# Attention on Trainium2: values of a head pair in one tall matmul, and a new order of the steps on TensorE

## The reference

```python
q, k, v = (split_heads(x @ W) for W in (W_query, W_key, W_value))
scores = einsum('hbqd,hbkd->hbqk', q, k)        # 64 x 64 for each sequence and head, not scaled
out = einsum('hbqk,hbkd->hbqd', softmax(scores), v)
return relu(merge_heads(out) + x @ W_res)       # [2048, 64, 128]
```

## Time and profile before

| | before |
|---|---|
| median of 3 runs | 1635.06 us |
| the profiled execution | 1633.92 us |
| its span (first to last instruction) | 1632.1 us |
| TensorE matmul busy | 1606.5 us, 98% of the span |
| TensorE weight load busy | 1541.2 us, 94% |
| VectorE, ScalarE, GpSimd busy | 1200.2, 1096.1, 932.6 us |
| granted TensorE clock over the span | 0.994 |

### The profile page before, as it was taken

The page is one execution under the profiler, slowest core; times in us unless marked ns, Lnnn a source line. Parts: engine busy times, 40 slices in busy tenths (PEclk is TensorE's granted clock), DMA queues, the critical chain, the costliest instruction groups (busy, mean ns, idle before and its releaser), DMA issues.

```text
span 1632.1 us, 95535 instructions
## 1 busy us (share of the span) xinstructions
PE 1606.5 (98%) x41984; PEld 1541.2 (94%) x41984; DVE 1200.2 (74%) x1537; ACT 1096.1 (67%) x1794; POOL 932.6 (57%) x1290
## 2 busy tenths in 40 slices
PE   6999999999999999999999999999999999999997
PEld 6999999999999999999999999999999999999996
DVE  4677777777777777777777777777777777777774
ACT  3676666667676766666676767666676767666664
POOL 2555555565655555565656555555656555555655
PEclk9999999999999999999999999999999999999998
DMA  2222222222223222222222232222222222322221
GB/s 59 76 83 89 83 85 84 84 84 84 84 84 88 83 87 84 84 84 84 84 84 86 83 89 83 86 84 84 84 84 84 84 88 82 88 84 84 84 84 54
DMA packets 271797, 135.33 MB, mean 83 GB/s; under 512 B 9312, under 2 KB 271712, under 8 KB 271712
## 3 DMA queue, kind: packets, MB, share of 16 engines
q1 hardware_dynamic: 270336, 134.25, 28.0%
q10 hardware_dynamic: 1376, 0.26, 0.1%
HBM read 67.37 MB, written 67.11 MB: 82 GB/s over the span
## 4 chain that ended last, share of the span: by engine, by line
PE 98%; issue 1%; DVE 0%; ACTq 0%; DMA 0%; ACT 0%; POOLq 0%; POOL 0%; DVEq 0%
PE ps_so L242 17%; PE ps_pt L231 16%; PE ps_so L220 13%; PE ps_qk L196 8%; PE ps_qk L198 8%; PE ps_qk L197 8%; PE ps_vr L209 8%; PE ps_vr L210 7%; PE ps_vr L211 7%; PE ps_x L186 7%; DMA w_raw<-in_L_rec_W_res_dram 0%; ACTq L334 0%; POOLq L39 0%; DVE attn L378 0%; DVE x_lo L351 0%
## 5 line engine op out<-in xcount | busy, mean ns | idle before, releaser
L150 POOL TENSOR_TENSOR y<-attn,vr 128x256 f32<-128x256 f32 x512 | 341.4, 688 | 596.3 <-issue 585.2
L308 ACT COPY probs_t<-ps_pt 128x512 f32<-128x512 f32 x512 | 302.0, 590 | 423.3 <-PE ps_pt L231 423.2
L362 DVE TENSOR_REDUCE row_max<-ps_so 128x16 f32<-128x1024 f32 x256 | 313.5, 1225 | 339.7 <-PE ps_so L242 339.5
L156 POOL TENSOR_SCALAR y<-y 128x512 f32<-128x512 f32 x256 | 380.7, 1487 | 22.4
L292 ACT COPY qk<-ps_qk 128x512 f32<-128x512 f32 x512 | 301.1, 588 | 65.0 <-PE ps_qk L198 13.9
L196 PE MATMUL ps_qk<-x_hi,w_hi 128*128 128x256 f32 x1024 | 332.7, 325 | 5.6 <-DVE x_lo L351 3.3
L231 PE MATMUL ps_pt<-ident,probs 128*128 128x128 f32 x2048 | 323.2, 280 | 0.8 <-ACT probs_t L308 0.7
L300 ACT COPY vr<-ps_vr 128x512 f32<-128x512 f32 x512 | 297.8, 582 | 33.8 <-PE ps_vr L211 1.5
L367 DVE TENSOR_TENSOR shifted<-ps_so,row_max 128x1024 f32<-128x1024 f32 x256 | 313.5, 1225 | 8.8
L209 PE MATMUL ps_vr<-w_hi,x_hi 128*128 128x256 f32 x1024 | 310.8, 304 | 0.1
L242 PE MATMUL ps_so<-vr,probs_t 64*64 64x33 f32 x8192 | 293.0, 222 | 4.2 <-issue 2.8
(11 more groups left out here) (23 smaller groups left out, 2249.0 us busy)
## 6 DMA issues: line engine op xcount, KB each, us to landing
x_in<-in_r_x_dram SPq DMA_DIRECT2D x256, 256.0 KB, 2.8
out_dram<-y SPq DMA_DIRECT2D x256, 256.0 KB, 2.3
w_raw<-in_L_rec_W_query_dram ACTq DMA_DIRECT2D x1, 64.0 KB, 3.1
w_raw<-in_L_rec_W_key_dram ACTq DMA_DIRECT2D x1, 64.0 KB, 3.7
w_raw<-in_L_rec_W_value_dram ACTq DMA_DIRECT2D x2, 32.0 KB, 3.2
w_raw<-in_L_rec_W_res_dram ACTq DMA_DIRECT2D x2, 32.0 KB, 2.5
```

Of the source, the lines that this page charges most:

```text
L150: nc.gpsimd.tensor_tensor(y[:, n % 2, a * HALF:(a + 1) * HALF].rearrange("k t (p j d) -> k j (t p) d", j=2, d=D), attn[:, n % 2, a * HALF: ...
L156: nc.gpsimd.tensor_scalar(y[:, n % 2], y[:, n % 2], 0.0, None, ALU.max).then_inc(y_ready, 1)
L362: nc.vector.reduce_max(row_max[:, :].rearrange("q (h u) -> q h u", h=HEADS), scores, AX_X).then_inc(max_ready, 1)
```

## The change

The matmuls of `weigh_values` get all 128 rows: both heads of a pair at once. For that the values of a pair are laid out on the diagonal: rows 0 to 63 have the first head's 33 columns and zeros beside them, rows 64 to 127 zeros and then the second head's 33 columns. That is `v_diag`, with one such layout for each of the two sequences. A matmul is now 128 rows by 64 output partitions with 66 columns, and there are 16 a body. The four results of a tile lie side by side in one bank, so that VectorE's views change (`inv_sum`, `heads`, `attn`). GpSimd fills `v_diag` with four copies a body in place of two and sets both buffers to zero at the start.

TensorE's step starts with `weigh_values(i-2)`, then `score(i)`; `transpose_x(i+2)` moves from before the last `project_vr` to behind the first `transpose_probs`; the waits for `shifted_ready`, `attn_ready`, `pt_ready` and `v_moved` that the next step's `weigh_values` needs stand inside the second `project_vr`, between its two tiles. VectorE's row maximum waits for the scores alone.

```diff
-        v_rows = [sb(f"v_rows{n}", [P, 2, HALF, PAIRS, VW]) for n in range(2)]
+        v_diag = [sb(f"v_diag{n}", [P, SEQS, 2, HALF, PAIRS, 2, VW]) for n in range(2)]
...
                     for j in range(2):
-                        other = slice((1 - j) * F, (2 - j) * F)
-                        nc.gpsimd.tensor_copy(
-                            v_rows[n % 2][j * F:(j + 1) * F].rearrange("k a t p d -> k a (t p d)"),
-                            vr[n][other, :, j].rearrange("k a t p d -> k a (t p d)")).then_inc(v_moved, 1)
-                        pool.wait_ge(v_moved, i * 2 + j + 1)
+                        for m, seq in enumerate((1 - j, j)):
+                            nc.gpsimd.tensor_copy(
+                                v_diag[n % 2][j * F:(j + 1) * F, seq, :, :, :, j].rearrange("k a t p d -> k a (t p) d"),
+                                vr[n][seq * F:(seq + 1) * F, :, j].rearrange("k a t p d -> k a (t p) d"),
+                            ).then_inc(v_moved, 1)
+                            if m == 0 or j == 1:
+                                pool.wait_ge(v_moved, i * 4 + j * 2 + m + 1)
...
+            for n in range(2):
+                last = nc.gpsimd.memset(v_diag[n][:, :, :, :, :, :, :], 0.0)
+            last.then_inc(diag_zero, 1)
+            pool.wait_ge(diag_zero, 1)
             pool.wait_ge(ident_zero, 1)
...
                     for p in range(PAIRS):
-                        for j in range(2):
-                            for s in range(SEQS):
-                                rows = slice(j * F, (j + 1) * F)
-                                at = (p * 2 + j) * BANK + O_AT + (a * HALF + t) * OW
-                                v = vr[n][rows, a, j, t, p, :] if s == j else v_rows[n % 2][rows, a, t, p, :]
-                                last = nc.tensor.matmul(
-                                    ps_so[s * F:(s + 1) * F, at:at + VW],
-                                    probs_t[rows, a, t * PAIRS + p, s * F:(s + 1) * F],
-                                    v, start=True, stop=True)
+                        for s in range(SEQS):
+                            at = (a * HALF + t) * BANK + O_AT + p * 2 * VW
+                            last = nc.tensor.matmul(
+                                ps_so[s * F:(s + 1) * F, at:at + 2 * VW],
+                                probs_t[:, a, t * PAIRS + p, s * F:(s + 1) * F],
+                                v_diag[n % 2][:, s, a, t, p].rearrange("k j d -> k (j d)"), start=True, stop=True)
...
             def step(i, n):
-                if has(i - 1):
-                    pe.wait_ge(shifted_ready, i)
-                if has(i - 3):
-                    pe.wait_ge(attn_ready, i - 2)
-                if has(i - 2):
-                    pe.wait_ge(pt_ready, halves(i - 2, 1))
-                    pe.wait_ge(v_moved, (i - 2) * 2 + 2)
-                if has(i):
-                    pe.wait_ge(qk_ready, halves(i, 1))
-                    score(i)
                 if has(i - 2):
                     weigh_values(i - 2, (n + 2) % RING, 0)
                     weigh_values(i - 2, (n + 2) % RING, 1).then_inc(o_done, 1)
+                if has(i):
+                    pe.wait_ge(qk_ready, halves(i, 1))
+                    score(i)
                 if has(i - 1):
                     pe.wait_ge(probs_ready, i)
                     transpose_probs(i - 1, 0)
+                if has(i + 2):
+                    transpose_x(i + 2, n)
                 if has(i + 1):
                     project_qk(i + 1, (n + 1) % RING, 0)
...
                 if has(i + 1):
                     project_qk(i + 1, (n + 1) % RING, 1)
-                if has(i + 2):
-                    transpose_x(i + 2, n)
-                if has(i):
-                    project_vr(i, n, 1)
+                if has(i):
+                    project_vr(i, n, 1, range(0, 1))
+
+                if has(i):
+                    pe.wait_ge(shifted_ready, i + 1)
+                if has(i - 2):
+                    pe.wait_ge(attn_ready, i - 1)
+                if has(i - 1):
+                    pe.wait_ge(pt_ready, halves(i - 1, 1))
+                    pe.wait_ge(v_moved, (i - 1) * 4 + 4)
+                if has(i):
+                    project_vr(i, n, 1, range(1, HALF))
...
                 if has(i):
                     dve.wait_ge(s_done, i + 1)
-                    if has(i - 2):
-                        dve.wait_ge(o_done, i - 1)
```

More of the change, by code:

```diff
@@ L69, in attention_program @@
         probs_t = sb("probs_t", [P, 2, HALF * PAIRS, P])
-        inv_sum = sb("inv_sum", [P, HEADS, TILES])
+        inv_sum = sb("inv_sum", [P, TILES, HEADS])
         attn = sb("attn", [P, 2, TILES, HEADS, D])
@@ L80, in attention_program @@
         ident_zero, ident_ready = sem("ident_zero"), sem("ident_ready")
-        ones_ready = sem("ones_ready")
+        ones_ready, diag_zero = sem("ones_ready"), sem("diag_zero")
         whi_ready, wlo_ready = sem("whi_ready"), sem("wlo_ready")
@@ L199, in project_qk, with project_vr @@
                 last.then_inc(qk_done, 1)
-            def project_vr(i, n, a):
-                if a == 1 or has(i - 1):
+            def project_vr(i, n, a, tiles=range(HALF)):
+                if tiles[0] == 0 and (a == 1 or has(i - 1)):
                     pe.wait_ge(vr_ready, halves(i, a) - 1)
@@ L205, in project_vr @@
                 w_vr_lo = w_lo[:, 2:4, :].rearrange("p w c -> p (w c)")
-                for t in range(HALF):
+                for t in tiles:
                     ps = ps_vr[:, t * 2 * COLS:(t + 1) * 2 * COLS]
@@ L211, in project_vr @@
                     last = nc.tensor.matmul(ps, x_lo[n][:, tok], w_vr_hi, start=False, stop=True)
-                last.then_inc(vr_done, 1)
+                if t == HALF - 1:
+                    last.then_inc(vr_done, 1)
             def score(i):
@@ L296, in copy_vr @@
                 if has(i - 4):
-                    act.wait_ge(v_moved, i * 2 - 6)
-                    act.wait_ge(o_done, i - 3)
+                    act.wait_ge(v_moved, (i - 4) * 4 + 4)
                     act.wait_ge(sum_ready, halves(i - 4, a))
@@ L356, in step @@
                 scores = bank[:, :, 0:O_AT].rearrange("q h (u f) -> q h u f", f=F)
-                heads = bank[:, :, O_AT:O_AT + TILES * OW].rearrange("q h (u d) -> q h u d", d=OW)
+                heads = bank[:, :, O_AT:O_AT + HEADS * VW].rearrange("q u (h d) -> q u h d", d=VW)
                 if has(i):
                     dve.wait_ge(s_done, i + 1)
-                    if has(i - 2):
-                        dve.wait_ge(o_done, i - 1)
                     nc.vector.reduce_max(row_max[:, :].rearrange("q (h u) -> q h u", h=HEADS), scores,
@@ L371, in step @@
                 if has(i - 2):
-                    if not has(i):
-                        dve.wait_ge(o_done, i - 1)
+                    dve.wait_ge(o_done, i - 1)
                     nc.vector.reciprocal(inv_sum[:, :, :], heads[:, :, :, D]).then_inc(inv_ready, 1)
@@ L378, in step @@
                     nc.vector.tensor_tensor(
-                        attn[:, n % 2].rearrange("q u h d -> q h u d"), heads[:, :, :, 0:D],
-                        inv_sum[:, :, :].unsqueeze(3).to_broadcast([P, HEADS, TILES, D]),
+                        attn[:, n % 2], heads[:, :, :, 0:D],
+                        inv_sum[:, :, :].unsqueeze(3).to_broadcast([P, TILES, HEADS, D]),
                         ALU.mult).then_inc(attn_ready, 1)
```

5 lines of the change are left out of this document (2 added, 3 removed).

## The result

The changed kernel takes 1651.29 us (4 runs, 1650.88 to 1651.46) against 1634.74 us of the kernel before beside it: a ratio of 1.0102, 95% interval 1.0085 to 1.012. It is slower by 1.0%. The profiled execution has a span of 1649.4 us, where the one before had 1632.1.

A forecast was written before the change was run, and what follows sets the result against it. TensorE, busy 98% of a 1632.1 us span, was the bound; 0.03 + 0.03 + 0.05 = 0.11 us a body, 28 us in 256, plus 1 us at the start gave span 1661, median 1664 us (1.8% slower), range 1625 to 1700.

The forecast's parts named there:

- Values +0.03: TensorE's value matmuls: same weight volume, doubled stream slightly longer than the loads, 0.96 against 0.93, +0.03 us a body.
- Rival C: Value matmuls: weight loads no longer hide under matmuls, +0.43 us a body, 1745 us, or about 2090; chance 6%.
- Switches +0.03: TensorE's three changes of tile shape: remain three, longer value records ahead of a switch add +0.03 us a body.
- rival B: Last project_vr to last value: drain-free switch (-0.09) or bare-rate loads (-0.08), faster, 1607 to 1627 us; chance 20%.
- Merged transposes 0: transpose_x beside the first transpose_probs: transposes cost nothing at their edges, so merging saves 0.
- Stall +0.05: TensorE's moved waits, between the second project_vr's tiles: late probs_t copy stalls 0 to 0.18 us a body, taken +0.05.
- GpSimd hidden: Two more v_diag copies a body, 0.43 us each: chain of 4.85 us in a period of 6.3 stays hidden.
- Start and end +1: Outside the bodies: two more memsets, 2 x 0.98 us, ahead of the identity cost 1 us at most, once.
- Another 3 us for the median: Whole run: 3 us added to the forecast span of 1661 to give the median of 1664 us.

The follow-up runs named there:

- e5: e1 with value matmuls that stream only 33 of the 66 columns in all bodies but the first (output not the reference's); 1618.34 us.
- e6: e1 with value matmuls that stream 132 columns, both pairs' diagonals at once (output not the reference's); 1851.92 us.
- e1: Changed kernel with the four waits back at the head of TensorE's step and the last project_vr in one piece; 1625.72 us, ratio to before 0.9947.
- e4: Kernel before with the 128-row value matmuls, diagonal values and views alone, order and waits as before; 1629.42 us, ratio to before 0.9971.
- e9: Changed kernel with only the wait for pt_ready moved to the head of the next step; 1625.74 us, ratio to before 0.9951.
- e2: Changed kernel with transpose_x back ahead of the last project_vr; 1632.37 us, ratio to before 0.9989.
- e7: e1 with the scores of tiles 0 and 1 ahead of the values and tiles 2 and 3 behind; 1635.84 us, ratio to before 1.0011.

## Why the prediction was right

It said 1664 us, between 1625 and 1700, slower. Measured were 1651. The body distance was forecast at 6.34 and is 6.342. That it fits so closely is in part luck: the switches were put 0.03 too high and the stall 0.036 too low, and the two cancel. The time is 12.7 us under the forecast because one term outside the body was missed.

- **Values +0.03.** Measured 0.938 against 0.916 from first to last record, +0.022. Same volume of weights, stream just above it: e5 and e6 bear out both. Rival C falls: it needs 1.36 us, so a load of 64 columns on all rows is hidden beneath the stream. The Trainium skill (TensorE: Matmul & The Clock Gate, Part 3, The mechanism) says in one place that loads overlap running matmuls only where row groups differ, and in another that a load into the background weight buffer may run ahead too. The first does not hold here: all records have the same rows and start 30 ns apart on average.
- **Switches +0.03.** Measured 0.507 before and 0.506 after for the three, 0. With 66 columns the record does not lengthen the step to the next shape; with the 132 of e6 it does, by 0.056. The step from full width to 128x64 is 0.209 as it was to 32x64, and half of rival B falls with it. The Trainium skill (TensorEngine Tiling (Array Packing), Key Properties) says that a change of tiling mode drains the engine; the 0.209 against 0.12 within one shape agrees.
- **Merged transposes 0.** e1 against e4, where the order of values and scores and the place of the transposes differ: 6.240 and 6.245. Right, to 0.005, which is little more than two traces of one kernel differ by.
- **Stall +0.05.** The mechanism was named: the copy of `probs_t`, 0.44 later, becomes the last of the waits, and the load behind it comes late. e9 shows that it alone does it, e2 that the moved transposes cause it. The size was 0.086 in the gap (0.102 of distance by e1), inside 0 to 0.18. The mis-sized piece is the time from the end of the copy to the load: I took 0.10 to 0.15 from rows at the edges, and in the loop it is 0.167 to 0.235, mean 0.217, inside the estimate's upper end.
- **GpSimd hidden.** Its copies take 408 ns each (403 ns before), and no row of TensorE waits for `v_diag` in the steady part.
- **Start and end +1.** This is the step that failed in size: the edge fell by 11.3 us, from 37.2 to 25.9. I had taken the 37 us from the trace as a lump and moved only the memsets in it. In it stood 11 us of slow bodies at the loop's entry and exit, whose rows named "issue". The sum, 256 x 0.112 = 28.6 less 11.3, is 17.3, the difference of the spans. The runs show that the pause at the exit goes with the old form of the values, and that form and order each remove part of those at the entry. What causes the pauses stays open; the ends of all of them follow a transfer of instructions by 1.26 to 1.68 us.
- **Another 3 us for the median.** The changed kernel's median is 1.9 us over the span of its trace, so 1.1 us of the miss lie here.

## What to carry to other kernels

A wait that is moved to an earlier place can lose the work that covered it: put it where the last semaphore has come by then, counted with the handling of the whole group of waits, here 0.17 to 0.37 us behind the event. Fewer and larger matmuls gain nothing in the steady body where the volume of weights sets the pace (6.230 before, 6.245 in e4), and zeros in the stream are free only up to the loads' time. Look at the bodies at the start and end one by one before you carry their total over, and at the instruction transfers beside them: what e1 gains over the kernel before, it gains there.

## Of the hardware, not expected

- The pace of the plain fp32 value records on 128 rows by 64 partitions agrees with 64 cycles a load, in turn over the two column tiles, or two cycles a column of stream in each tile side by side, whichever is longer, plus some ns a matmul: 33, 66 and 132 columns gave bodies of 6.213, 6.240 and 7.127 us and first to last value records 0.903, 0.938 and 1.745 us apart.
- 64 score records in a row take 0.696 us from first to last in every kernel here, whatever stands ahead of them, the first 32 of them 0.27; in two groups of 32 (e7) each takes 0.27.
- A change of tile shape takes 0.209 us from start to start behind a full matmul of 256 columns, and 0.147 to 0.151 behind the records of 33, 64 or 66 columns in the kernels before and after, to whatever shape. It is not the same everywhere: 0.206 behind 132 columns (e6), and 0.243 from the full matmul to the scores in e7.
